# The feature sum of a block is turned in a place of the count banks' rotation

## What is computed

```python
src_h = h[src] @ W_msg.T + b_msg
msg = src_h + edge_embed[clip(edge_type, 0, 8)]
messages = segment_sum(msg, dst, num_segments=12500)
h_new = gru_cell(messages, h, W_ih, W_hh, b_ih, b_hh)
return layernorm(x + h_new)
```

## Time and profile before

| | |
|---|---|
| median of three runs | 1253.09 us |
| the profiled execution's own time | 1256.97 us |
| its span, first to last instruction | 1255.1 us |
| TensorE busy | 1037.9 us, 83% |
| VectorE busy | 859.2 us, 68% |
| GpSimd busy | 733.5 us, 58% |
| ScalarE busy | 660.5 us, 53% |
| mean granted clock of TensorE | 0.926 |

### The profile page before, as it was taken

One profiled execution on the slowest core, in us unless ns is written; L12 is line 12 of the kernel. 1 busy time (PEld: TensorE's weight loads), 2 busy tenths in 40 slices (PEclk: granted clock), 3 DMA queues, 4 the chain that ended last, 5 costly groups with the idle time before them and its releaser, 6 DMA issues.

```text
span 1255.1 us, 23526 instructions
## 1 busy us (share of the span) xinstructions
PE 1037.9 (83%) x8411; PEld 656.5 (52%) x8411; DVE 859.2 (68%) x2699; ACT 660.5 (53%) x1283; POOL 733.5 (58%) x779
## 2 busy tenths in 40 slices
PE   5456677888888988989889989889888888888884
PEld 2124354555555555556556656555555555555552
DVE  8413557677776877868777767777876777676644
ACT  4243404455655555656666656555655556554622
POOL 7725645665566666666666666566666666566640
PEclk9566568999999999999999999999998999999996
DMA  8529311222222322322333223223323233332321
GB/s 244 159 79 310 107 33 53 78 77 74 74 77 79 91 77 77 91 78 77 82 83 92 79 78 92 74 79 92 90 77 89 76 89 83 86 92 80 83 81 28
DMA packets 94565, 114.23 MB, mean 91 GB/s; under 512 B 19820, under 2 KB 80616, under 8 KB 94441
## 3 DMA queue, kind: packets, MB, share of 16 engines
q0 software_dynamic: 35264, 73.19, 21.8%
q1 hardware_dynamic: 57320, 37.79, 10.2%
q10 hardware_dynamic: 1856, 1.66, 0.5%
HBM read 96.56 MB, written 16.00 MB: 90 GB/s over the span
## 4 chain that ended last, share of the span: by engine, by line
PE 64%; issue 10%; DVE 9%; ACT 7%; another core or an unknown queue 7%; DMA 1%; SPq 1%; DVEq 0%; ACTq 0%
PE psf L1097 28%; PE psb L1082 14%; PE pAB L1026 5%; PE psg L1065 4%; PE pAB L1040 4%; ACT mem L1213 3%; DVE ohl L868 2%; PE pAB L1043 2%; DVE ohk L862 2%; PE psg L1069 2%; PE psf L1102 1%; DMA arena<-in_x 1%; ACT mem L1153 1%; DVE ohk L865 1%
## 5 line engine op out<-in xcount | busy, mean ns | idle before, releaser
L604 POOL DMA_INDIRECT xg<-x_split,idx x648 | 616.1, 951 | 392.1 <-PE psg L1069 151.0
L1213 ACT CAST mem<-psb 128x432 f16<-128x432 f32 x896 | 426.7, 525 | 398.4 <-PE psb L1082 300.8
L1097 PE MATMUL psf<-mem 128*128 128x384 bf16 (+1 forms) x2744 | 618.4, 330 | 13.6 <-issue 6.8
L1082 PE MATMUL psb<-ohk,ohl 128*128 128x108 bf16 (+3 forms) x1865 | 421.6, 264 | 97.9 <-issue 57.4
L862 DVE TENSOR_TENSOR ohk<-table_bank,prm 128x392 bf16<-128x392 f16 (+3 forms) x437 | 271.0, 620 | 108.6 <-PE psb L1082 69.1
L1097 PEld LDWEIGHTS psf<-mem 128*128 128x128 f16 (+1 forms) x2744 | 240.4, 99 | 131.3 <-issue 34.9
L1082 PEld LDWEIGHTS psb<-ohk,ohl 128*128 128x128 bf16 x1865 | 173.6, 100 | 251.3 <-issue 116.4
L868 DVE TENSOR_TENSOR ohl<-table_bank,prm 128x512 bf16<-128x512 f16 x437 | 180.8, 414 | 0.0
L891 DVE TENSOR_TENSOR mem<-mem,psg 128x136 f32 (+9 forms) x184 | 54.9, 298 | 168.4 <-remote 106.8
L604 POOL DMA_INDIRECT xg<-in_x,idx x88 | 84.2, 957 | 76.3 <-PE psg L1069 44.7
L865 DVE TENSOR_TENSOR ohk<-table_bank,sort 128x40 bf16<-128x40 f16 (+3 forms) x437 | 106.5, 244 | 0.0
(11 more groups left out here) (148 smaller groups left out, 808.4 us busy)
## 6 DMA issues: line engine op xcount, KB each, us to landing
xg<-x_split,idx POOLq DMA_INDIRECT x648
x_split<-mem SPq DMA_DIRECT2D x24, 384.0 KB
xb<-in_xT SPq DMA_DIRECT2D x49, 128.0 KB
arena<-in_x SPq DMA_DIRECT2D x24, 256.0 KB
arena<-in_xN SPq DMA_DIRECT2D x47, 128.0 KB
out<-spill SPq DMA_DIRECT2D x19, 128.0 KB
out<-arena SPq DMA_DIRECT2D x144, 8.0 KB
out<-arena SPq DMA_DIRECT2D x15, 128.0 KB
```

The costliest lines, as they stand in the source:

```text
L604: pool.indirect_dma_start(out=xg[:, p % RING, :] if split else xg32(p % RING), out_offset=None, in_=x_d if split else x, in_offset=bass.In ...
L1082: ins = pe.matmul(psb[:, bank % NB, held * HC:(held + m) * HC], ohl[:, e % KB, :], ohk[:, e % KB, d * HC:(d + m) * HC], start=(k == 0), st ...
L1097: pe.matmul(psf[:, 0:3 * H], Bb[q % 2][0:kk, HT + h, :], xs[0:kk, h, :, :].rearrange("p c f -> p (c f)"), start=(h == 0), stop=(h == HI - ...
L1213: act.copy(Bb[q % 2][:, :, n:n + MOST], psb[:, bank % NB, 0:MOST * HC].rearrange("p (d h) -> p h d", h=HC)).then_inc(S["s_eb"], 1)
```

## The change

It does five things.

- The nine type matmuls leave the last feature item and follow the turn in T. `s_fd` is incremented by the block's last feature matmul.
- T's output no longer goes to `psf` but to a place of its own in the rotation of the three `psb` banks: columns 0 to 127 for the turned sum, 128 to 255 for the types. C evicts that place and counts in `s_eb`; `s_cp` is gone. A new function, `rotation`, numbers the count banks and the turns in the order in which `ITEMS` fills them (896 + 28 places).
- The first feature item of block q + 1 waits for `s_sc` of block q (S) instead of C.
- The eviction of block q + 2's first bank waits for `s_tt` (T of block q, with its types) instead of `s_fd`.
- In the order, S moves from position 0.02 to 0.01, the first feature item from 0.17 to 0.06; T and C, before at 0.06 and 0.10, come together, behind the first slot at or after 0.10 that completes a bank.

```diff
-SETTLED = (0.02, 0.06, 0.10)
-CLEAR = 0.17
+SUMMED = 0.01
+TURNED = 0.10
+CLEAR = 0.06
...
+CLOSED = frozenset(e for e in range(SLOTS_N) if BANK_LAST[pieces(e)[-1][0]] == e)
...
-                       [(at, u) for at, (_, u) in zip(SETTLED, late)])
+                       [(SUMMED, u) for _, u in late[:1]])
+        if late:
+            k = next(k for k, (at, u) in enumerate(mixed) if at >= TURNED and (not own or u[0] == "B" and u[1] in CLOSED))
+            mixed[k + 1:k + 1] = [(mixed[k][0], u) for _, u in late[1:]]
...
+def rotation():
+    banks, turns, evicted = {}, {}, []
+    for it in ITEMS:
+        if it[0] == "B":
+            for b, _, _, _ in pieces(it[1]):
+                banks.setdefault(b, len(banks) + len(turns))
+            evicted += [banks[b] for b, _, _, _ in pieces(it[1]) if BANK_LAST[b] == it[1]]
+        elif it[0] == "T":
+            turns[it[1]] = len(banks) + len(turns)
+        elif it[0] == "C":
+            evicted.append(turns[it[1]])
+    assert evicted == list(range(BANKS + NQ))
+    return banks, turns
...
                         if f == 0:
-                            pe.wait_ge(S["s_eb"], (q + 1) * FB // MOST)
+                            pe.wait_ge(S["s_eb"], BANK_AT[(q + 1) * FB // MOST - 1] + 1)
                             if q == 0:
                                 pe.wait_ge(S["s_xl"], UNITS)
                             else:
-                                pe.wait_ge(S["s_cp"], q)
+                                pe.wait_ge(S["s_sc"], q)
...
                         if f == PARTS - 1:
-                            for t in range(NT):
-                                ins = pe.matmul(psf[:, 3 * H:3 * H + FB], sel[:, NT - 1 - t:NT - 1 - t + P], Bb[q % 2][:, t, :], start=False,
-                                                stop=(t == NT - 1), skip_group_check=True)
                             ins.then_inc(S["s_fd"], 1)
                     elif it[0] == "T":
                         q = it[1]
+                        at = TURN_AT_BANK[q]
                         pe.wait_ge(S["s_sc"], q + 1)
-                        pe.matmul(psf[:, 0:FB], added[:, :], ident[:, :], start=True, stop=True, skip_group_check=True
-                                  ).then_inc(S["s_tt"], 1)
+                        pe.wait_ge(S["s_eb"], at - NB + 1)
+                        pe.matmul(psb[:, at % NB, 0:FB], added[:, :], ident[:, :], start=True, stop=True,
+                                  skip_group_check=True)
+                        for t in range(NT):
+                            ins = pe.matmul(psb[:, at % NB, FB:2 * FB], sel[:, NT - 1 - t:NT - 1 - t + P], Bb[q % 2][:, t, :],
+                                            start=False, stop=(t == NT - 1), skip_group_check=True)
+                        ins.then_inc(S["s_tt"], 1)
...
                             if q >= 2 and n == 0:
-                                act.wait_ge(S["s_fd"], q - 1)
+                                act.wait_ge(S["s_tt"], q - 1)
...
-                        act.copy(cnts[0:ND2, 0, o:o + FB], psf[0:ND2, 3 * H:3 * H + FB])
-                        act.copy(den[:, o:o + FB], psf[:, 0:FB]).then_inc(S["s_cp"], 1)
+                        at = TURN_AT_BANK[q] % NB
+                        act.copy(cnts[0:ND2, 0, o:o + FB], psb[0:ND2, at, FB:2 * FB])
+                        act.copy(den[:, o:o + FB], psb[:, at, 0:FB]).then_inc(S["s_eb"], 1)
```

## The result

The changed kernel takes 1261.83 us (median of 20 runs, 1252.32 to 1273.26) where the kernel before takes 1254.66 (20 runs): 1.0058 of it, 95% interval 1.003 to 1.0086. It is slower by about 0.5%. I had forecast 1253 us and no change, with a line of 0.5% between no change and slower: the result lies just beyond that line, and I had given slower a chance of 0.25.

The account below looks back on a forecast made before the run. TensorE's work and idle time were taken to bound the kernel. The terms -12.3 + 3.7 + 8 + 1 - 0.7 = -0.3 us gave 1252.8 for the median, forecast as 1253 us, range 1238 to 1267.

Parts of the forecast that it names:

- What bounds the kernel: Whole kernel: TensorE's work and idle time make up the time; it is busy 83% of the span.
- The held eviction, 8 us: Behind the turn, TensorE waits for the first bank's later eviction: 0.42 us in each of 19 blocks, 8 us lost.
- the rotation chokes: Rival: turn and two held banks fill all three psb places, from about 0.9 us delay; 1267 us, chance 0.19.
- The rest of the sum: Terms besides the held eviction: -12.3 us for C, +3.7 for S, +1 for the spread, -0.7 at the end.
- The wait for C goes, 12.3 us: Ahead of the feature matmuls: the first features no longer follow the copies C; 12.3 us gained.
- my third rival: First feature matmul waits for its own block's last bank's eviction: 0.3 us more in 27 blocks, 1261 us, chance 0.10.
- The wait for S moves, 3.7 us lost: The features instead of the turn wait for the sum S; 3.7 us lost, bounds -1.3 and +8.5.
- The turn in the rotation, nothing: The turn waits for the eviction three places back, a bank complete before this block's features began; costs nothing.
- The spread, 1 us lost: Features lie on 94% of a block instead of 83%; 1 us lost, bounds -8 and +10.
- The clock: TensorE's clock is at the upper level, 2.4 GHz, in most windows; no clock is to be won.
- The prompt signal: Rival: the last feature matmul's signal comes promptly, the wait for S falls to some 5 us; 1226 us, chance 0.05.
- My own sign for the choke: If idle time ahead of the count matmuls rises by over 15 us, the rotation chokes.

Follow-up runs that it names:

- experiment 1: Changed kernel with types reading a constant and the first eviction waiting for s_fd, so no held eviction: 1245.56 us, 0.9911 of the kernel before.
- experiments 9 and 10: Third chip, against the kernel before: the changed kernel again, 1.0052; the changed kernel with types reading a constant and no held eviction, 0.9922.
- experiments 1, 3 and 4: Changed kernel with, in turn: no held eviction, 1245.56 us; the turn at 0.08 inside the second bank, 1247.12 us; S moved to 0.0, 1252.25 us.
- experiments 5 to 8: Prompt chip: changed kernel without both waits 0.9859, also with CLEAR = 0.17 0.985, with turn and S moved 0.9885; kernel before with S moved 0.9962.
- experiments 9 to 12: Third chip, late signals, against the kernel before: changed kernel 1.0052, without held eviction 0.9922, with turn and S moved 0.9889, without both waits 0.9846.
- 13 to 16: Fourth chip, late signals: changed kernel without both waits 0.9872, also with CLEAR = 0.17 0.9916; kernel before with S first 0.9986; changed kernel 1.0036.
- experiment 15: Kernel before with only S moved, from 0.02 to 0.0, right behind the last feature item, on a late chip: 0.9986 of the kernel before.

## Why the prediction was wrong, step by step

- **What bounds the kernel:** right. All that moved the time was TensorE's idle time, and, which I had ruled out with "no clock is to be won", its clock.
- **The held eviction, 8 us: this step failed.** Taken away, it gave back 1.3% to 1.5%, 17.3 and 18.0 us of the dense stretch in two pairs. I had taken "0.42 each, near the lower end"; by the timeline TensorE stood 0.97 us on average, 18.4 us in 19 blocks. I took the prompt row of block 10 for all blocks; it is the common case, but five signals that are 2.0 to 2.3 us late make two thirds of the idle time. The mean delay was 0.77 us and not 0.03. I had 0.9 us as the point from which the rotation chokes, and gave that rival 0.19: its mechanism is what happened, at about four fifths of its price.
- **The rest of the sum:** about right as a whole. Without its 8 us for the hold, my sum says 8.3 us less than the kernel before; the changed kernel without the hold measured 0.9911 and 0.9922 of it, 10 to 11 us less. That is in part luck: the next two terms and the clock, each off by some us, cancel.
- **The wait for C goes, 12.3 us:** right in kind; no feature matmul waits for C. But the same matmuls keep 17 to 28 us of idle time even without the wait for S, from the last bank's eviction and unnamed causes. That was my third rival's mechanism, at work as a lesser term.
- **The wait for S moves, 3.7 us lost:** right in kind. 35.2 us stand ahead of the features, where I expected about 30; less what the kernel without that wait keeps there (17.2), S has 18 us of it, so less than I thought is S and more is the last bank's eviction and what has no name. I had VectorE waiting for TensorE at S in 11 of the blocks, and in half of the other 17 held by work that itself waits for TensorE; in the trace it comes to S straight from other work in all blocks but one. In block 19, which I put at 1 us, the wait was 3.15.
- **The turn in the rotation, nothing:** not contradicted, not tested apart.
- **The spread, 1 us lost:** not contradicted, not isolated.
- **The clock:** missed. Of what the hold costs, 9.6 of 17.3 us (experiment 1) and 6.6 of 18.0 us (experiments 9 and 10) are the same matmuls at the lower level of the clock. A sum of idle times alone could not have given it.
- **The prompt signal** (the completion tail of the Trainium skill, TensorE: Matmul & The Clock Gate, The cost: per-tile semaphore tail): on the chips with late signals the trace contradicts it by 1 us and more. On the prompt chip it agrees to within 0.1 us: the signal comes 0.01 us beyond the shown ends. What the change is worth there wasn't run.

Two groups of rows were read wrongly. At block 20 it wasn't a late signal that held up the copy. ScalarE was busy from 949.86 up to it, with an eviction, the loading of a table and an activation:

```profile
949.86 0.52 ACT L1213 CAST mem<-psb 128x432 f16<-128x432 f32 x1 [2.15 <-issue]
...
950.40 1.28 ACT L1198 ACT_TABLE_LOAD   x1
...
951.69 0.30 ACT L1198 ACTIVATE sd<-mv,eps 128x2 f32<-128x2 f32 x1
```

What spoke for late signals were the rows of blocks 17 and 11. And the windows of the earlier trace rows miss most of the 31 us that the dense stretch spends at the lower level of the clock.

My own sign for the choke was that the idle time ahead of the count matmuls rises by over 15 us; over the whole run it rose by 14.0. Over the dense stretch alone, the rows are, before and after:

```profile
L1082 PE MATMUL psb<-ohk,ohl 128*128 128x108 bf16 (+3 forms) x1697 | 384.8, 259 | 70.2 <-issue 45.0 <-ACT mem L1213 14.5 <-DVE ohl L868 8.9
...
L1108 PE MATMUL psb<-ohk,ohl 128*128 128x108 bf16 (+3 forms) x1694 | 385.2, 260 | 86.3 <-issue 54.4 <-ACT mem L1242 24.6 <-DVE ohl L893 5.8
```

The ledger of this stretch: turn and features together waited 37.5 us and now 34.7, so only 2.8 us were gained there where I had 12.3 less 3.7. Ahead of the count matmuls 16.1 us more, not 9. Ahead of all other matmuls 5.4 us less. That is 7.8 us of idle time, and with 2.9 us of busy time 10.7 us, the growth of the stretch in these two traces. The medians differ by 7.2 us.

## What to carry to other kernels

A buffer that is given back later is paid for where the rotation is short: count what lies between the late release and the next instruction that needs it, against all the delays of such signals in the trace and not the shortest: a few long ones can make most of the sum. If that is one item, put the release inside work that needs no new place, here into an open bank: that gave back 1.2% of the 1.5% that the hold had cost. A sum of idle times can miss the clock: in experiments 1, 3 and 4 the idle time fell by 3 to 8 us and the busy time of the same matmuls by 10. Whether one long wait is worse than the same time in short ones isn't shown: the kernel before has a single wait over 2 us in its stretch and yet 31 us at the lower level.

## What the runs showed of the hardware

**TensorE's signals can come late after the shown ends of its matmuls, and whether they do depends on the chip.** In the trace of the kernel before from which the rows ahead of the prediction come, a sparse group is shown as over at 587.91, and VectorE, idle, adds its result 1.80 us later:

```profile
587.62 0.29 PE L1069 MATMUL psg<-ohs,tohb 128*128 128x68 bf16 x4
...
589.71 0.30 DVE L891 TENSOR_TENSOR mem<-mem,psg 128x136 f32 x1 [1.89 <-remote]
```

On the chip of experiments 5 to 8, in the kernel before with S moved, 0.14 us pass:

```profile
542.48 0.29 PE L1069 MATMUL psg<-ohs,tohb 128*128 128x68 bf16 x4
...
542.91 0.30 DVE L891 TENSOR_TENSOR mem<-mem,psg 128x136 f32 x1 [0.65 <-PE psg L1069]
```

Over all 184 groups the semaphore's event lies a median of 1.2 us behind the shown end (a tenth over 2.9) in that trace, 1.2 to 1.5 us in those of experiments 9 to 12, 0.9 to 1.7 in 13 to 16, and 0.01 in 5 to 8. Since the shown ends are modelled, the trace can't tell whether the matmuls or the signals are late. The mean durations of the costliest groups of VectorE, ScalarE and GpSimd agree within 2%. The kernel before takes 1255 and 1275 us on two of the late chips and 1084 us on the prompt one. With S moved, TensorE is busy there for 849.90 of 881.50 us of the dense stretch:

```profile
158.30:1039.80 881.50, 849.90 (x7632) 567.57 (x7630) 721.62 (x2296) 574.41 (x1107) 613.99 (x648) 1.00 0.34 94
```

The same kernel on the late chip of experiment 15:

```profile
211.30:1206.10 994.80, 880.54 (x7632) 567.75 (x7630) 725.83 (x2295) 564.53 (x1107) 606.50 (x640) 0.99 0.31 82
```

TensorE is idle for 32 us on the one and 114 us on the other, and 31 us longer busy. The kernel before takes some 170 us longer on a late chip, over twenty times what this change moved. The late signals go with that difference; that they make all of it is argued and not shown, and what makes them late isn't known.
